# Two images packed into one float32r convolution, in the first phase of a binary-convolution and gated-FFN block

## What is computed

```python
x = x + _L0_conv_ref(_ln_c(x), w, b, gamma, beta)   # (1)
t = _to_tokens(x)
t = t + _L0_ffn_ref(_ln_t(t), ...)                  # (2)
# _L0_conv_ref(x, w, b, gamma, beta):
xa = sign_a(x)
wc = jnp.clip(w - jnp.mean(w, axis=1, keepdims=True), -1.0, 1.0)
wq = sign_w(wc) * alpha                             # one alpha per output channel
y = conv_general_dilated(xa, wq, (1, 1), padding=[(1, 1), (1, 1)]) + b
mean, var = over images and pixels                  # batch norm over all 32 images
return relu((y - mean) * rsqrt(var + EPS) * gamma + beta)
```

## Time and profile before

| | |
|---|---|
| median of 3 runs | 2095.73 us (2092.15 to 2099.53) |
| the profiled execution | 2102.06 us |
| its span in the trace | 2100.1 us |
| PE, DVE, ACT, POOL busy | 1961.1, 1600.5, 1216.2, 938.0 us |
| first convolution matmul starts | 19.92 us |
| statistics of the last chunk start | 472.13 us |
| first work of the second phase (ReLU, L594) starts | 477.43 us |

### The profile page before, as it was taken

How to read it: one execution, slowest core, us unless ns; L and a number is a source line. 1 busy time by engine, 2 the same in 40 slices (tenths; PEclk the granted TensorE clock), 3 DMA queues, 4 the chain that set the end, 5 groups by cost and what they waited for, 6 DMA issues and landing times.

```text
span 2100.1 us, 35007 instructions
## 1 busy us (share of the span) xinstructions
PE 1961.1 (93%) x9515; PEld 961.7 (46%) x9515; DVE 1600.5 (76%) x4580; ACT 1216.2 (58%) x2030; POOL 938.0 (45%) x714
## 2 busy tenths in 40 slices
PE   6999999994999999999999999999999999999995
PEld 2444444442444444444444444444444444444442
DVE  4766666665788888888888888887888888878875
ACT  3555555544666666666666666666656666655652
POOL 1000000005465565566555566655656566555543
PEclk9999999996999999999999999999999999999998
DMA  6787877852133333333333333333333333333223
GB/s 251 279 297 283 301 291 288 295 215 73 52 141 117 115 116 132 114 126 117 126 112 135 116 112 120 135 113 113 130 119 117 123 115 122 116 112 129 96 76 119
DMA packets 78097, 318.24 MB, mean 152 GB/s; under 512 B 23561, under 2 KB 28610, under 8 KB 74050
## 3 DMA queue, kind: packets, MB, share of 16 engines
q1 hardware_dynamic: 64626, 265.07, 34.5%
q10 hardware_dynamic: 13392, 52.33, 6.7%
HBM read 237.88 MB, written 78.26 MB: 151 GB/s over the span
## 4 chain that ended last, share of the span: by engine, by line
PE 48%; DMA 11%; SPq 6%; DVE 4%; issue 4%; POOL 1%; ACT 1%; ACTq 0%; POOLq 0%; DVEq 0%
PE ps L1063 24%; DMA y<-y_int 6%; PE ps L1052 6%; PE ps L1054 5%; PE ps L1053 5%; PE ps L1008 5%; SPq L429 4%; DMA w_row<-wrow 3%; PE ps L1041 2%; DMA wse<-w_row 2%; SPq L435 1%; POOL rm L489 1%; ACT hs L566 1%; SPq L440 1%; DVE rm L776 1%
## 5 line engine op out<-in xcount | busy, mean ns | idle before, releaser
L1063 PE MATMUL ps<-hs,w_c 128*128 128x448 f32 x1792 | 765.1, 555 | 0.6 <-ACT yo L576 0.6
L566 ACT ACTIVATE hs<-ps,b1c,undo 128x448 f32<-128x448 f32 x896 | 609.3, 719 | 129.0 <-PE ps L1054 125.3
L1063 PEld LDWEIGHTS ps<-hs,w_c 128*128 128x128 f32 x1792 | 314.6, 191 | 211.3 <-issue 177.2
L965 PE MATMUL ps<-yo,cwT 128*128 128x448 bf16 x2016 | 396.2, 357 | 3.9 <-ACT y L544 3.9
L470 POOL TENSOR_TENSOR xb<-xb,zr 128x448 f32<-128x448 f32 x224 | 261.1, 1168 | 271.9 <-ACT zr L594 254.9
L475 POOL TENSOR_TENSOR tl<-tr,th 128x448 f16<-128x448 f32 x224 | 245.4, 1097 | 306.9 <-PE ps L1054 185.8
L1052 PE MATMUL ps<-th,w_h 128*128 128x448 f16 x896 | 318.7, 356 | 25.3 <-ACT hs L566 25.3
L1054 PE MATMUL ps<-th,w_l 128*128 128x448 f16 x896 | 316.3, 353 | 0.0
L1053 PE MATMUL ps<-tl,w_h 128*128 128x448 f16 x896 | 316.3, 353 | 0.0
L482 POOL TENSOR_TENSOR yo<-yo,base 128x448 f32<-128x448 f32 x224 | 281.3, 1262 | 77.4 <-DVE yo L885 77.4
L965 PEld LDWEIGHTS ps<-yo,cwT 128*128 128x128 bf16 x2016 | 193.8, 98 | 214.4 <-issue 24.9
(11 more groups left out here) (143 smaller groups left out, 2086.1 us busy)
## 6 DMA issues: line engine op xcount, KB each, us to landing
xb<-x SPq DMA_DIRECT2D x21, 1568.0 KB, 7.4
xb<-x SPq DMA_DIRECT2D x33, 896.0 KB, 4.7
gate_all<-gate_row ACTq DMA_DIRECT2D x32, 896.0 KB, 4.5
result<-yo SPq DMA_DIRECT2D x32, 896.0 KB, 3.5
y_int<-y SPq DMA_DIRECT2D x32, 784.0 KB, 4.1
xb<-x SPq DMA_DIRECT2D x33, 672.0 KB, 4.4
gate_all<-gate_row ACTq DMA_DIRECT2D x32, 672.0 KB, 5.6
result<-yo SPq DMA_DIRECT2D x32, 672.0 KB, 3.0
```

What stands on the lines that cost most here:

```text
L566: nc.scalar.activation(hs[(b + slot) % 2][:, j, :], ps[:, H_BANK + j, 0:T], ACT.Gelu_apprx_tanh, bias=b1c[:, j:j + 1], scale=undo[:, 1:2]) ...
L965: last = M(bank, cwT[:, t, :], sg[b][:, c * ROWS + dy:c * ROWS + dy + ROWS, dx:dx + SIDE], start=t == 0, stop=t == TAPS - 1)
L1063: last = M(bank, w2_c[:, j, :], hs[(b + c) % 2][:, j, :], start=first, stop=final)
```

## The change

The first phase now takes images in pairs p = 0 to 15 (NP = 16). In short:

- Centring: every chunk of every image is multiplied on PE by the centring matrix in plain float32 (`centre`, one product each for image 1 and image 0 of the pair, two PSUM banks). The constant MEAN_FROM is 99, so that the code for means (`token_means`, `copy_mean`, `level`, `level_last`, `save_mean`) never runs. The split into float32r parts is gone.
- Packing: ACT takes the sign of both images from PSUM, multiplies the second's by 3072 (`scaled`), and POOL adds the two into the float32r tile `packs`.
- Convolution: one per pair, with float32r weights; three PSUM banks in turn.
- Unpacking: ACT writes 1/3072 of the sum, rounded to int16 (`take_high`); DVE subtracts 3072 times that from the sum, which gives the other image (`decode`).
- Statistics, stores of y and loads of x go on as before, for two images at a time; images 30 and 31 are now one pair. y of the odd images is int16.

```diff
-        cwT = sb("cwT", [C, TAPS, C], bf16)
+        cwT = sb("cwT", [C, TAPS, C], f32r)
...
+            def store_y(p, part):
+                sp.wait_ge(decoded, p * NCH + (HALF, NCH)[part])
+                for b in range(2):
+                    sp.dma_start(y_dram[b][p * C:(p + 1) * C, PART[part]], y16[b][:, PART[part]]
+                                 ).then_inc(y_saved[part], 16)
...
+            def pack(q, c):
...
+                pool.wait_ge(signed, signs_upto(q, c, 0))
+                pool.wait_ge(scaled, q * NCH + c + 1)
+                first, second = (sgn[k][(q * NCH + c) % 2][:, :].rearrange("p (r w) -> p r w", w=SIDE) for k in range(2))
+                nc.gpsimd.tensor_tensor(pk[q % 2][:, 1 + c * ROWS:1 + (c + 1) * ROWS, 1:1 + SIDE], second, first,
+                                        ALU.add).then_inc(packed, 1)
...
+            def sign(q, c):
+                for k in (1, 0):
...
+                        act.wait_ge(centred, centres_upto(q, c, k))
+                        z = ps[:, CEN_BANK + k, 0:T]
+                    chunk = q * NCH + c
+                    wait_count(act, packed, chunk - 1)
+                    nc.scalar.activation(sgn[k][chunk % 2][:, :], z, ACT.Sign).then_inc(signed, 1)
+                act.wait_ge(signed, signs_upto(q, c, 1))
+                nc.scalar.activation(sgn[1][chunk % 2][:, :], sgn[1][chunk % 2][:, :], ACT.Copy,
+                                     scale=PACK).then_inc(scaled, 1)
...
+            def take_high(p, c):
+                chunk = p * NCH + c
+                act.wait_ge(conv_done, chunk + 1)
...
+                nc.scalar.activation(cut(y16[1], c), ps[:, V_BANK + chunk % V_RING, 0:T], ACT.Copy,
+                                     scale=1.0 / PACK).then_inc(high_taken, 1)
...
+            def decode(p, c):
+                chunk = p * NCH + c
+                dve.wait_ge(high_taken, chunk + 1)
...
+                V.scalar_tensor_tensor(cut(y16[0], c), cut(y16[1], c), -PACK, ps[:, V_BANK + chunk % V_RING, 0:T],
+                                       ALU.mult, ALU.add).then_inc(decoded, 1)
...
+            batch_stats(NP - 2, NCH - 1)
             dve.wait_ge(bn_taken, EARLY * NCH)
             V.bn_aggr(bn_early, bnst[:, 0:EARLY * NCH, :])
-            phase1(n_img - 1, (n_img - 1) % 6, (n_img - 1) // 6)
-            batch_stats(n_img - 1, (n_img - 1) % 2, NCH - 1)
+            phase1(NP - 1)
+            batch_stats(NP - 1, NCH - 1)
...
+            def centre(q, c):
+
+                for k in (1, 0):
+                    if k and (c == 0 or c == HALF):
+                        pe.wait_ge(x_in_s[q % 2][c // HALF], 32 * (q // 2 + 1))
+                    before = centred_before(q, c)
+                    if before[0] >= 0:
+                        pe.wait_ge(signed, signs_upto(*before, k))
+                    M(ps[:, CEN_BANK + k, 0:T], kt[:, K_CEN:K_CEN + C], cut(xs[(2 * q + k) % 4], c),
+                      start=True, stop=True).then_inc(centred, 1)
...
+            def conv(p, c):
+                chunk = p * NCH + c
+                pe.wait_ge(packed, p * NCH + min(c + 2, NCH))
+                wait_count(pe, decoded, chunk - V_RING + 1)
+                bank = ps[:, V_BANK + chunk % V_RING, 0:T].rearrange("p (r w) -> p r w", w=SIDE)
                 for t in range(TAPS):
                     dy, dx = divmod(t, 3)
-                    last = M(bank, cwT[:, t, :], sg[b][:, c * ROWS + dy:c * ROWS + dy + ROWS, dx:dx + SIDE],
+                    last = M(bank, cwT[:, t, :], pk[p % 2][:, c * ROWS + dy:c * ROWS + dy + ROWS, dx:dx + SIDE],
                              start=t == 0, stop=t == TAPS - 1)
...
+            for p in range(NP):
                 for c in range(NCH):
-                    conv(n, i % 2, c)
...
+                    conv(p, c)
+                    for q, d in centres_at(p, c):
+                        centre(q, d)
```

More of the change, by code:

```diff
@@ L214, in block_kernel @@
         border_clear = sem("border_clear")
-        x_in_s = [sem(f"x_in{b}") for b in range(3)]
+        x_in_s = [[sem(f"x_in{b}_{part}") for part in range(2)] for b in range(2)]
+        packed = sem("packed")
+        scaled = sem("scaled")
+        high_taken = sem("high_taken")
+        decoded = sem("decoded")
         mean_done = sem("mean_done")
@@ L218, in block_kernel @@
         mean_saved = sem("mean_saved")
[L219 removed]
+        mean_in = [sem(f"mean_in{b}") for b in range(4)]
         levelled = sem("levelled")
[L221 to L222 removed]
+        levelled_last = sem("levelled_last")
         centred = sem("centred")
@@ L225, in block_kernel @@
         conv_done = sem("conv_done")
-        y_copied = sem("y_copied")
         bn_taken = sem("bn_taken")
-        y_saved = [sem(f"y_saved{b}") for b in range(2)]
+        y_saved = [sem(f"y_saved{part}") for part in range(2)]
         coef_ready = sem("coef_ready")
@@ L289, in pairs, with signs_upto, by_mean, centres_upto @@
                 body(n, n % 2)
[L291 to L315, removed]
+        def signs_upto(q, c, k):
+            return q * 2 * NCH + 2 * c + 2 - k
+        def by_mean(q, c):
+            return q >= MEAN_FROM and c < HALF
+        def centres_upto(q, c, k):
+            if q < MEAN_FROM:
+                return signs_upto(q, c, k)
+            return MEAN_FROM * 2 * NCH + (q - MEAN_FROM) * 2 * (NCH - HALF) + 2 * (c - HALF) + 2 - k
+        def centred_before(q, c):
+            if c > (HALF if q >= MEAN_FROM else 0):
+                return q, c - 1
+            return q - 1, NCH - 1
+        FIRST_CENTRES = ([(0, 4)], [(0, 5)], [(0, 6)], [(1, 0)], [(1, 1), (1, 2)], [(1, 3), (1, 4)], [(1, 5), (1, 6)])
+        FIRST_SIGNS = ([(0, 2), (0, 3)], [(0, 4)], [(0, 5)], [(0, 6)], [(1, 0)], [(1, 1), (1, 2)], [(1, 3), (1, 4)])
+        def centres_at(p, c):
+            if p == 0:
+                return FIRST_CENTRES[c]
+            return [(p + 1, c)] if p + 1 < NP and not by_mean(p + 1, c) else []
+        def signs_at(p, c):
+            if p == 0:
+                return FIRST_SIGNS[c]
+            if c == 0:
+                return [(1, 5), (1, 6)] if p == 1 else [(p, NCH - 1)]
+            return [(p + 1, c - 1)] if p + 1 < NP else []
+        def mean_cut(n, c):
+            return cut(yo[n % 2], c) if n % 4 > 1 else hs[n % 2][:, c, :]
         def is_int(n):
@@ L368, in _ @@
                              ).then_inc(params_in, 16)
+            for part in range(2):
+                load_pair(1, part)
             def load_x(n, b, part):
@@ L373, in load_y @@
             def load_y(n, b, part):
-                sp.dma_start(y16[b][:, PART[part]], y_dram[bass.ds(n * C, C), PART[part]]
+                sp.dma_start(y16[b][:, PART[part]], y_dram[b][bass.ds((n - b) * (C // 2), C), PART[part]]
                              ).then_inc(xy_in[b][part], 16)
[L377 to L398, removed]
-                if has(n + 2):
-                    save_mean(n + 2, i % 2)
-                sp.wait_ge(y_copied, (n + 1) * NCH)
-                sp.dma_start(y_dram[bass.ds(n * C, C), :], y16[i % 2][:, :]).then_inc(y_saved[i % 2], 16)
@@ L411, in _ @@
+            sp.wait_ge(signed, 2 * HALF)
+            load_pair(2, 0)
+            for p in range(NP):
+                phase1(p)
+            store_y(NP - 1, 1)
+            for part in range(2):
+                sp.wait_ge(y_saved[part], 32 * NP)
+                sp.wait_ge(bn_taken, (NP - 1) * 2 * NCH + 2 * (HALF, NCH)[part])
+                for b in range(2):
                     load_y(b, b, part)
@@ L553, in _ @@
+            for p in range(NP):
+                for c in range(NCH):
+                    for q, d in signs_at(p, c):
+                        sign(q, d)
+                    take_high(p, c)
+                if p == 0:
+                    nc.scalar.activation(cwa, cwc, ACT.Abs, accum_out=abs_sum).then_inc(abs_summed, 1)
             act.wait_ge(coef_ready, 2)
```

297 lines of the change are left out of this document (152 added, 145 removed).

## The result

| | before | after |
|---|---|---|
| median | 2096.05 us (4 runs) | 2030.72 us (4 runs, 2029.77 to 2031.63) |
| ratio | | 0.9689, 95% interval 0.9671 to 0.9707 |
| profiled execution, its span | 2102.06, 2100.1 us | 2029.77, 2028.0 us |
| first convolution matmul | 19.92 us | 27.24 us |
| statistics of the last chunk end | 472.76 us | 410.43 us |

The changed kernel is 65.3 us faster; 69.8 were forecast. The first phase ends 62.65 us earlier by these two profiles; the 2.7 us more between the medians are within that scatter of the second phase. The second phase, from the first ReLU to the end, whose code is the same, took 1613 to 1628 us in the profiles of this study (1621.5 in a second profile of the changed kernel), so the 9.5 us between the two above are its own scatter: the same changed kernel shows 1613.2 and 1621.5.

What follows compares the result with a forecast made beforehand. PE was taken to bound the first phase. Pair 15 starts at 26.3 + (364 - 12.6) + 5 = 382.7 us, statistics end at 403.0 instead of 472.8: gain 69.8 us, forecast 2026 us, range 2006 to 2056.

Steps and rivals of the forecast that it cites:

- Part 1: Convolution on PE: 1008 instead of 2016 matmuls, in float32r at 0.200 us each, 202 us in all.
- rival (a): Packed convolution: float32r weight load does not hide, 0.379 us per matmul, 180 us more, 2206 us; 4 in 100.
- The weight load: Packed convolution on PE: the 191 ns float32 weight load hides under a matmul streaming for 0.188 us.
- Part 2: Centring on PE: a float32 product of 0.752 us per chunk and image adds 162 us; means, 51 us, go.
- Part 3: Other engines in a 3.30 us slot: ACT 2.2, DVE 1.9 to 2.1, POOL 1.10 us; added PE waits cost nothing.
- (b): Centring banks hand over too late: at 0.3 us for each of some 105 slots, 31 us, 2057 us; 8 in 100.
- (c): Packing or unpacking becomes the bound: at 3.8 us for a slot, 52 us more, 2078 us; 2 in 100.
- (d): Last pair's tail hides: 12.6 + 1.9 instead of 20.3 us, 6 us less, 2020 us; within the forecast's range, no separate chance.
- Part 4: Start: first convolution at 26.3 us instead of 19.92, later by 6 us, behind four float32 products and the weights' signs.
- the cold clock and a wait: After the first convolution: lower clock level and a short wait for the squares' sum, 5 us, between 2 and 9.
- Part 5: Last pair bound by DVE, with the merge of 30 images before it: 20.3 us, taking back 6 to 8 us.
- the sign named for it: Profile sign for the last pair: PE waiting for DVE there, for some 8 us.

Runs made afterwards that it cites:

- the short taps: Changed kernel with eight of nine convolution matmuls per chunk on 5 rows (280 columns) instead of 8 (448): 1967.52 us.
- the cheap centring: Changed kernel with each float32 centring product replaced by one bfloat16 identity pass over the upper halves of x: 1928.44 us, ratio 0.919.

## Why the prediction was right

- **The bound, and that the gain is PE's work.** Right: PE is busy for 300 of 300 us after the change, and work taken off PE came out of the time nearly whole (66.5 of 71 us with the short taps, 103.6 of 121 with the cheap centring).
- **Part 1, the float32r matmul.** The term that was mis-sized: 0.211 us, not 0.200, 11 us in all, within the stated bounds of 0.19 and 0.22. The row I read it from was of contiguous columns, and even there a stream costs 0.205. The convolution's rows of 56 add 0.006. I had the rows in rival (a), as a second pass, and set them aside because bfloat16 shows none. It shows no second pass, but it was no measure of the small price that float32r pays for rows.
- **The weight load.** It hides, as forecast, and not because the matmul above it is as long: its record can be longer than the distance of the matmuls it lies under.
- **Part 2, the centring.** Right: 0.376 us for a pass, 1.50 us for a chunk of both images.
- **Part 3, the others.** Right: POOL 1.04 us per packing, DVE 0.62 for a decoding; no hand-over shows on PE in the steady part. Rivals (b) and (c) did not come; nor did (d), by the 19.7 us of the last pair.
- **Part 4, the start.** 27.24 against 26.3. The 5 us for the cold clock and a wait were too many: from 27.24, 945 x 0.211 + 162.4 us lead to 389.0, and pair 15 starts at 390.77, so 1.7 us. The granted clock was 0.61 from 20 to 30 us and 1.00 from 30 us on, so the lower level ended soon after the first convolution began; I had read its length from the row of before, 0.86 from 20 to 40 us.
- **Part 5, the last pair.** 19.7 against 20.3, with the mechanism as described; moving the merge took 3.5 us off. Only the sign named for it was off: PE waits 1.74 us by its row, not some 8.
- **The sum.** First ReLU at 414.78 where 407.6 was implied: 10.4 (float32r up to pair 15) + 0.9 (start) - 3.3 (clock and wait) - 0.6 (last pair) - 0.3 (what follows it) = 7.1 us. The time was only 4.7 us over the forecast. The start and the clock's share made up for 2.4 of the 10.4 us of the mis-sized term, and between the medians the rest of the kernel was 2.7 us shorter, which nothing in the change explains: that part of the agreement is luck.

## What to carry to other kernels

Where PE is the bound and its operands hold few distinct values, two problems in one float32r matmul nearly halve its work: 0.211 us instead of two times 0.192. What it takes (packing, unpacking) should lie on engines that have room, as here. Price such a product from a row with the same access pattern, since the type's cost depends on it. And before a waiting step is moved back in a queue, look at what stands behind it in that same queue: here the saving of two mean rows held back a store of y by 6.7 us instead of 2.5, and the engine that mattered stopped for it, three queues on. Where the profile gives no reason for a wait, or one long past, compare its end with the landings of the transfers that the code waits for.

## What the runs showed of the hardware that was not expected

A float32r matmul of 448 columns costs 0.205 us in contiguous columns and 0.211 to 0.213 in 8 rows of 56, at a pitch of 58 or of 64, where bfloat16 takes 0.192 with the same rows and float16 0.189 in contiguous columns. Full-array weight loads with records of 0.189 us ran under matmuls 0.132 us apart without a stall. The second phase, unchanged, took 1613 to 1628 us from profile to profile.
